# A gated cross-attention kernel on one core: own queries and keys projected for two batches at once

## The reference, cut to what matters

```
x = x + tanh(g_xattn[1]) * L1_xattn(layernorm(x), ctx)       # ctx: 16 x 361 x 256
def L1_xattn(x, xa, ...):                                    # 16 heads of width 16
    q, k, v    = split(x  @ Wqkv     + bqkv)                 # own queries, keys, values: 100 a batch
    qa, ka, va = split(xa @ Wqkv_aux + bqkv_aux)             # context keys and values: 361 a batch
    p  = softmax(q @ k.T  / sqrt(16));  pa = softmax(q @ ka.T / sqrt(16))
    out = p @ v * (1 - gate) + pa @ va * gate
    return out @ Wo + bo
```

## Time and profile before

| what | value |
|---|---|
| median of three runs | 1337.34 us (1335.42 to 1337.89) |
| the profiled execution | 1332.8 us, span 1331.1 us |
| PE, DVE, ACT, POOL busy over the span | 89%, 45%, 37%, 31% |
| second attention's step, from t = 3 to t = 13 | about 23.4 us |
| PE busy between 640 and 926 us | 281.21 of 286 us, granted clock 0.99 |

### The profile page before, as it was taken

One profiled execution on the slowest core, in us unless ns is written; L12 is line 12 of the kernel. 1 busy time (PEld: TensorE's weight loads), 2 busy tenths in 40 slices (PEclk: granted clock), 3 DMA queues, 4 the chain that ended last, 5 costly groups with the idle time before them and its releaser, 6 DMA issues.

```text
span 1331.1 us, 29074 instructions
## 1 busy us (share of the span) xinstructions
PE 1183.8 (89%) x11408; PEld 919.2 (69%) x11408; DVE 598.1 (45%) x1351; ACT 486.7 (37%) x1143; POOL 411.9 (31%) x428
## 2 busy tenths in 40 slices
PE   5999999866999999668899999999989979999960
PEld 3667777645999999535566666666656769999960
DVE  4777776752201101364566666565453402222215
ACT  2445555412333232123444444444442212233321
POOL 3666666612222221211001100110110225555532
PEclk9999999967999999957899999999989989999985
DMA  5011114017999997401100101000000129999965
GB/s 165 24 39 32 30 31 124 8 38 285 335 325 320 332 332 285 138 25 37 45 13 19 31 13 30 19 19 2 8 14 27 53 91 350 352 351 354 337 236 167
DMA packets 64352, 180.92 MB, mean 136 GB/s; under 512 B 10137, under 2 KB 36569, under 8 KB 55769
## 3 DMA queue, kind: packets, MB, share of 16 engines
q1 hardware_dynamic: 56008, 155.07, 34.2%
q0 software_dynamic: 8064, 22.03, 4.5%
q10 hardware_dynamic: 144, 1.97, 0.4%
HBM read 163.11 MB, written 15.93 MB: 135 GB/s over the span
## 4 chain that ended last, share of the span: by engine, by line
PE 67%; POOL 11%; issue 9%; DVE 7%; DMA 3%; ACT 1%; SPq 1%; POOLq 0%; DVEq 0%; ACTq 0%
PE kept_psum L1982 16%; PE kept_psum L1991 15%; POOL at_sum L316 6%; PE kept_psum L1222 5%; PE kept_psum L1278 5%; PE kept_psum L2007 4%; PE kept_psum L1242 4%; PE kept_psum L1675 4%; PE kept_psum L1264 3%; PE kept_psum L1191 3%; PE kept_psum L1206 3%; POOL at_sum L319 2%; DVE at_negmax L961 2%; PE kept_psum L1971 1%; POOL at_vn L327 1%
## 5 line engine op out<-in xcount | busy, mean ns | idle before, releaser
L1934 ACT ACTIVATE ex_hT<-kept_psum,ex_w 128x128 f32<-128x128 f32 x464 | 132.3, 368 | 309.2 <-PE kept_psum L1982 309.2
L1982 PE MATMUL kept_psum<-ex_xT,ex_w 128*128 128x128 f32 x1856 | 223.7, 277 | 0.0
L1982 PEld LDWEIGHTS kept_psum<-ex_xT,ex_w 128*128 128x128 f32 x1856 | 216.9, 194 | 0.1
L1991 PE MATMUL kept_psum<-ex_w,ex_hT 128*128 128x256 f32 x928 | 214.0, 380 | 0.0
L1991 PEld LDWEIGHTS kept_psum<-ex_w,ex_hT 128*128 128x128 f32 x928 | 170.5, 191 | 19.3
L1769 POOL DMA_INDIRECT ex_results<-ex_yt,ex_to_row x84 | 82.8, 986 | 256.1 <-DVE ex_yt L1907 256.1
L1104 ACT ACTIVATE at_probs<-kept_psum 120x800 f32<-120x800 f32 (+2 forms) x128 | 101.2, 842 | 85.2 <-PE kept_psum L1248 85.1
L961 DVE TENSOR_REDUCE at_negmax<-kept_psum 100x2 f32<-100x722 f32 x128 | 115.3, 901 | 0.0
L520 ACT ACTIVATE at_probs<-kept_psum 120x800 f32<-120x800 f32 (+1 forms) x96 | 80.2, 836 | 71.8 <-PE kept_psum L632 71.6
L1907 DVE TENSOR_TENSOR ex_yt<-kept_psum,ex_b 128x256 f32<-128x256 f32 x32 | 13.6, 424 | 200.6 <-PE kept_psum L1991 200.6
L1764 POOL DMA_INDIRECT ex_xt<-ex_normed,ex_from_row x84 | 81.5, 970 | 68.9 <-DVEq L1896 32.8
(11 more groups left out here) (239 smaller groups left out, 1782.7 us busy)
## 6 DMA issues: line engine op xcount, KB each, us to landing
ex_w<-in_pack_in SPq DMA_DIRECT2D x32, 1028.0 KB, 6.1
ex_w<-in_pack_out SPq DMA_DIRECT2D x32, 1024.0 KB, 7.6
ex_w<-in_pack_in SPq DMA_DIRECT2D x52, 514.0 KB, 5.3
ex_w<-in_pack_out SPq DMA_DIRECT2D x52, 512.0 KB, 6.1
at_ctx<-in_ctxT SPq DMA_DIRECT2D x32, 361.0 KB, 3.5
ex_normed<-ex_xhat SPq DMA_DIRECT2D x16, 200.0 KB
ex_xhat<-ex_results SPq DMA_DIRECT2D x8, 400.0 KB
ex_shT<-ex_results SPq DMA_DIRECT2D x8, 400.0 KB
```

The costliest lines, as they stand in the source:

```text
L1934: last = act.activation(hT[t % N][:, c, :], ps_h[:, (t * U + u) % N, i * P:(i + 1) * P], ACT.Gelu, bias=w1[t % N][:, B1 + c:B1 + c + 1])
L1982: last = pe.matmul(ps_h[:, (t * U + u) % N, i * P:(i + 1) * P], w1[t % N][:, c * ff + f:c * ff + f + P], xT[t % N][:, c, :], start=(c == 0 ...
L1991: last = pe.matmul(ps_y[:, t % N, 0:D], hT[t % N][:, c, :], w2[t % N][:, c * D:(c + 1) * D], start=(c == 0), stop=(c == FC - 1))
```

## The change

Own queries and keys are projected in even steps only, for batches t+2 and t+3 together. The ring's order gets `xT` twice in a row (t+2 and t+3, ahead of `sum_aux`), and `own` becomes two uses, `queries` at the old place and `own_keys` after `value01`. Each is half of the blocks, with 200 moving columns instead of 100. In odd steps none of these uses exists. On ScalarE both `take_xT` stand where the one stood, `take_queries` (four activations of 200 columns) stands at the place of `take_own`, and `take_own_keys` (two activations of 200 columns) behind the exponents of unit 2. The buffers of keys and queries go from three to four and lie in one tile each, those of xT hold two batches each, two of them. `Early` projects the context keys of four batches instead of three, so key0 and key1 start with batch 4, in step t = 2.

```diff
-EARLY_BYTES = 40960
+EARLY_BYTES = 44672
 class Early:
-    NC, NK = 4, 3
+    NC, NK = 4, 4
...
-    ORDER = (("max", 0), ("key0", 2), ("key1", 2), ("sum_main", -1), ("turn_main", -2), ("xT", 2), ("sum_aux", -1),
-             ("turn_aux", -2), ("own", 2), ("value01", 0), ("mixT", -2), ("value2", 0), ("out", -2),
+    ORDER = (("max", 0), ("key0", 2), ("key1", 2), ("sum_main", -1), ("turn_main", -2), ("xT", 2), ("xT", 3), ("sum_aux", -1),
+             ("turn_aux", -2), ("queries", 2), ("value01", 0), ("own_keys", 2), ("mixT", -2), ("value2", 0), ("out", -2),
              ("value_own", 0))
...
+    OF_TWO = ("xT", "queries", "own_keys")
+    def used(name, t, off):
+        if name in OF_TWO and t % 2:
+            return False
+        return on(t + off) and (name, t + off) not in ahead and not (name in ("key0", "key1") and t + off < NK)
...
+        def take_queries(p):
+            act.wait_ge(ready["queries"], p + 1)
+            act.wait_ge(masks_set, 4)
+            need(act, by_key_ready, (2 * p + 2 - NK) * UNITS)
             for i in range(KC):
                 for a in range(2):
-                    act.activation(qz[b % NK][:, i, a, :], bank[:, i * T:(i + 1) * T], ACT.Identity, bias=bqm[:, i, a:a + 1], scale=own[:, a:a + 1])
+                    last = act.activation(qz[:, two_of(p), i, a, :], by_two("queries", p, i), ACT.Identity, bias=bqm[:, i, a:a + 1], scale=own[:, a:a + 1])
+            last.then_inc(taken["queries"], 1)
+
+        def take_own_keys(p):
+            act.wait_ge(ready["own_keys"], p + 1)
+            need(act, by_key_ready, (2 * p + 2 - NK) * UNITS)
             for i in range(KC):
-                last = act.activation(kT[b % NK][:, i, 0:T], bank[:, (KC + i) * T:(KC + i + 1) * T], ACT.Identity, bias=bqk[:, KC + i:KC + i + 1])
-            last.then_inc(taken["own"], 1)
+                last = act.activation(kT[:, two_of(p), i, 0:T], by_two("own_keys", p, i), ACT.Identity, bias=bqk[:, KC + i:KC + i + 1])
+            last.then_inc(taken["own_keys"], 1)
...
-            if on(t + 2):
+            if on(t + 2) and t % 2 == 0:
                 take_xT(t + 2)
+                take_xT(t + 3)
             if on(t - 1):
                 take_sum(t - 1, 1)
-            if on(t + 2):
-                take_own(t + 2)
+            if on(t + 2) and t % 2 == 0:
+                take_queries((t + 2) // 2)
...
             if on(t):
                 exponents(t, 2)
+            if on(t + 2) and t % 2 == 0:
+                take_own_keys((t + 2) // 2)
...
+        def project_two(name, p):
+            bank = into(name, p)
+            first_of = KC * ("queries", "own_keys").index(name)
+            if name == "queries":
+                pe.wait_ge(taken["xT"], 2 * p + 2)
+            for i in range(KC):
+                at = (first_of + i) * P
                 for c in range(KC):
-                    last = pe.matmul(bank[:, i * T:(i + 1) * T], w[:, c, i * P:(i + 1) * P], xT[b % NX][:, c, :], start=(c == 0), stop=(c == KC - 1))
-            last.then_inc(ready["own"], 1)
+                    last = pe.matmul(bank[:, i * 2 * T:(i + 1) * 2 * T], w[:, c, at:at + P], xT[p % (NX // 2)][:, c, :, :].rearrange("p b t -> p (b t)"),
+                                     start=(c == 0), stop=(c == KC - 1))
+            last.then_inc(ready[name], 1)
...
-            if on(t + 2):
+            if on(t + 2) and t % 2 == 0:
                 turn_x(t + 2)
+                turn_x(t + 3)
...
-            if on(t + 2):
-                project_own(t + 2)
+            if on(t + 2) and t % 2 == 0:
+                project_two("queries", (t + 2) // 2)
             if on(t):
                 by_key(t, 2)
             if on(t) and t >= PRE:
                 values01(t)
+            if on(t + 2) and t % 2 == 0:
+                project_two("own_keys", (t + 2) // 2)
```

More of the change, by code:

```diff
@@ L726, in __init__ @@
         self.ctxt = [m.sb(f"ctx{i}", [P, KC, S]) for i in range(self.NC)]
-        self.kT = [m.sb(f"kT{i}", [P, KC, T + S]) for i in range(self.NK)]
+        self.kT = m.sb("kT", [P, self.NK, KC, T + S])
         self.ctx_loaded = [m.sem(f"ctx_loaded{i}") for i in range(self.NC)]
@@ L815, in attend1 @@
     HH, HS = H // HALVES, H // STRIPS
-    NC, NK, NX, PRE = early.NC, early.NK, 3, 2
+    NC, NK, NX, PRE = early.NC, early.NK, 4, 2
+    TWOS = B // 2
     KEYS = T + S
@@ L828, in attend1 @@
     xhat = [m.sb(f"xhat{i}", [T, D]) for i in range(2)]
-    xT = [m.sb(f"xT{i}", [P, KC, T]) for i in range(NX)]
-    qz = [m.sb(f"qz{i}", [P, KC, 2, T]) for i in range(NK)]
+    xT = [m.sb(f"xT{i}", [P, KC, 2, T]) for i in range(NX // 2)]
+    qz = m.sb("qz", [P, NK, KC, 2, T])
     shift = m.sb("shift", [P, HS, T], BF16)
@@ L842, in attend1 @@
     rden_ready, mixed_ready, mix_ready = m.sem("rden_ready"), m.sem("mixed_ready"), m.sem("mix_ready")
-    ORDER = (("max", 0), ("key0", 2), ("key1", 2), ("sum_main", -1), ("turn_main", -2), ("xT", 2), ("sum_aux", -1),
-             ("turn_aux", -2), ("own", 2), ("value01", 0), ("mixT", -2), ("value2", 0), ("out", -2),
+    ORDER = (("max", 0), ("key0", 2), ("key1", 2), ("sum_main", -1), ("turn_main", -2), ("xT", 2), ("xT", 3), ("sum_aux", -1),
+             ("turn_aux", -2), ("queries", 2), ("value01", 0), ("own_keys", 2), ("mixT", -2), ("value2", 0), ("out", -2),
              ("value_own", 0))
-    ready = {n: m.sem(f"{n}_ready") for n, _ in ORDER}
-    taken = {n: m.sem(f"{n}_taken") for n, _ in ORDER}
-    x_ready = taken["out"]
+    OF_TWO = ("xT", "queries", "own_keys")
     STEPS = range(-2, B + 4)
     ahead = [(n, b) for b in range(PRE) for n in ("value01", "value2")]
-    ring = ahead + [(n, t + off) for t in STEPS for n, off in ORDER if on(t + off) and (n, t + off) not in ahead
-                    and not (n in ("key0", "key1") and t + off < NK)]
+    def used(name, t, off):
+        if name in OF_TWO and t % 2:
+            return False
+        return on(t + off) and (name, t + off) not in ahead and not (name in ("key0", "key1") and t + off < NK)
+    ring = ahead + [(n, (t + off) // 2 if n in OF_TWO[1:] else t + off) for t in STEPS for n, off in ORDER if used(n, t, off)]
+    ready = {n: m.sem(f"{n}_ready") for n in dict(ORDER)}
+    taken = {n: m.sem(f"{n}_taken") for n in dict(ORDER)}
+    x_ready = taken["out"]
     ring_at = {use: i for i, use in enumerate(ring)}
@@ L1077, in take_key @@
             need(act, by_key_ready, (b - NK + 1) * UNITS)
-            act.activation(kT[b % NK][:, i, T:KEYS], ring_bank(name, b)[:, 0:S], ACT.Identity, bias=bka[:, i:i + 1]).then_inc(taken[name], 1)
+            act.activation(kT[:, b % NK, i, T:KEYS], ring_bank(name, b)[:, 0:S], ACT.Identity, bias=bka[:, i:i + 1]).then_inc(taken[name], 1)
         def take_xT(b):
@@ L1082, in take_xT, with two_of, by_two @@
             need(act, ready["value_own"], b - NX + 1)
-            act.activation(xT[b % NX][:, :, :], ring_bank("xT", b)[:, 0:KC * T].rearrange("p (c t) -> p c t", c=KC),
+            act.activation(xT[b // 2 % (NX // 2)][:, :, b % 2, :], ring_bank("xT", b)[:, 0:KC * T].rearrange("p (c t) -> p c t", c=KC),
                            ACT.Copy).then_inc(taken["xT"], 1)
-        def take_own(b):
-            act.wait_ge(ready["own"], b + 1)
+        def two_of(p):
+            return slice(2 * p % NK, 2 * p % NK + 2)
+        def by_two(name, p, i):
+            return ring_bank(name, p)[:, i * 2 * T:(i + 1) * 2 * T].rearrange("p (b t) -> p b t", t=T)
+        def take_queries(p):
+            act.wait_ge(ready["queries"], p + 1)
             act.wait_ge(masks_set, 4)
-            need(act, by_key_ready, (b - NK + 1) * UNITS)
-            bank = ring_bank("own", b)
+            need(act, by_key_ready, (2 * p + 2 - NK) * UNITS)
             for i in range(KC):
                 for a in range(2):
-                    act.activation(qz[b % NK][:, i, a, :], bank[:, i * T:(i + 1) * T], ACT.Identity, bias=bqm[:, i, a:a + 1], scale=own[:, a:a + 1])
+                    last = act.activation(qz[:, two_of(p), i, a, :], by_two("queries", p, i), ACT.Identity, bias=bqm[:, i, a:a + 1], scale=own[:, a:a + 1])
[3 more added lines that the diff above has]
+            need(act, by_key_ready, (2 * p + 2 - NK) * UNITS)
             for i in range(KC):
-                last = act.activation(kT[b % NK][:, i, 0:T], bank[:, (KC + i) * T:(KC + i + 1) * T], ACT.Identity, bias=bqk[:, KC + i:KC + i + 1])
-            last.then_inc(taken["own"], 1)
+                last = act.activation(kT[:, two_of(p), i, 0:T], by_two("own_keys", p, i), ACT.Identity, bias=bqk[:, KC + i:KC + i + 1])
+            last.then_inc(taken["own_keys"], 1)
         def exponents(b, u):
@@ L1211, in by_query @@
             if u == 0:
-                pe.wait_ge(taken["own"], b + 1)
+                pe.wait_ge(taken["queries"], b // 2 + 1)
+                pe.wait_ge(taken["own_keys"], b // 2 + 1)
                 if b < NK:
@@ L1221, in by_query @@
                 rows = slice(32 * strip, 32 * strip + 32)
```

(8 more changed lines are left out.)

2 lines of the change are left out of this document (1 added, 1 removed).

## The result

The changed kernel takes 1342.8 us in the median of eight runs, the kernel before 1335.9 in eight runs beside it: a ratio of 1.0054, 95% interval 1.0032 to 1.0076, so slower by 7 us (4 to 10). The forecast was +8.2 us, and the profile after shows the two waits where they were expected.

The account below looks back on a forecast made before the run. TensorE's list of groups was taken to bound the kernel. Steps 2 to 13 at +8.9 us, step 1 at -1.9 and steps -2 to 0 at +1.2 gave +8.2, so 1345.5 us, range 1336 to 1351.

Parts of the forecast that it names:

- The even steps' wait: In steps 2, 4 to 12 sum_aux waits for ScalarE's copy of xT, 1.40 us longer than before.
- The odd steps' wait: In steps 3, 5 to 13 k2 waits for VectorE's maxima; q2 to k2 takes 2.44 us, the step saves 1.18.
- a pair's +1.5 us: Even plus odd step: 1.4 us waiting for ScalarE, 1.0 for VectorE, 0.6 saved, half a microsecond no longer overlapped.
- The projection group: Eight TensorE instructions of 200 columns take 1.56 us, bounds 0.93 and 1.92; a pair of batches saves 0.60 us.
- The sum: Steps 2 to 13: six even steps at +2.66 us and six odd at -1.18 give +8.9 us.
- Steps -2 to 1: Start of the second attention: steps -2 to 0 cost +1.2 us, step 1 gains 1.9 us.
- another clock in steps -2 to 2: Sign of a wrong prediction: TensorE's clock in these steps differs from the one assumed, 0.50 in steps -2 to 0.
- the start runs at a better clock: Rival: denser TensorE in steps 0 and 2 raises the clock sooner, 3 to 8 us off the forecast; 15 in 100.
- key0 gives nothing: Step 1: k0 waits for VectorE anyway, so removing key0 saves no time.
- The falling clock: Rival: new gaps drop TensorE's clock in the six even steps, +18.6 us on top, 1364 us; 10 in 100.
- Step 14: Already without xT and own, used as the model for odd steps; no cost of its own in the sum.
- The total: Whole kernel: +8.2 us, 1345.5 us on the median of 1337.3; routing and experts only move with the attention.

Follow-up runs that it names:

- experiment 1: The changed kernel with the second xT of an even step moved behind sum_aux, in the ring, on TensorE and on ScalarE: ratio 1.0012 to the kernel before.
- experiment 4: The kernel before with only xT moved ahead of turn_main, in the ring and on TensorE, in every step: ratio 1.0338.
- Experiment 2: The changed kernel with the first half of value01 moved ahead of k2 in steps without a projection: ratio 0.9987 to the kernel before.
- experiment 3: The changed kernel with both the second xT behind sum_aux and value01 split around k2: ratio 0.9983 to the kernel before, 0.9971 when repeated.
- Experiments 4 to 6: experiment 4; the same with ScalarE's copy of xT between the halves of exponents(1), 1.0141; the changed kernel with three short copies ahead of take_xT, 1.0120.
- early keys alone: The kernel before with early keys of four batches and four buffers, nothing else: ratio 0.9995.

## Why the prediction was right

**The even steps' wait** was sized at 1.40 us and measured 1.35; experiment 1 shows it as a cause by taking it out, and experiment 4 by adding it to the kernel before, where a shorter one came along. **The odd steps' wait** for VectorE's maxima, read off step 14 at 2.44 us, is 2.39; an odd step gains 1.23 us where 1.18 was forecast. Experiment 2 shows that there was idle time to fill. (In the forecast's account of a pair's +1.5 us the last part should be the transposes' 0.32, not half a microsecond: 1.40 + 1.0 - 0.60 - 0.32 = 1.48. The sum doesn't use it.)

**The projection group** was the mis-sized term: eight instructions of 200 columns take 753.46 to 754.91 = 1.45 us, not 1.56. The straight line between 100 and 256 columns was too high in the middle. So the pair saved 0.8 us rather than 0.6. In the queries' place 0.1 of it is lost again: value01 starts 1.16 behind k2, not 1.05, since it has caught up with VectorE's normalization, which ends at 756.01; value01's own 1.82 us, not 1.92, give that back. From q2 to q3 it is 7.32 us against 7.53 in the forecast. An even step costs 2.40 instead of 2.66.

**The sum** over steps 2 to 13 came to +6.1 us instead of +8.9: six even steps at 0.26 less each make 1.6 of that, the odd ones 0.3, and steps 2 and 3 are a further 0.8 below the pattern.

**Steps -2 to 1** were forecast at -0.7 us together and measured -1.6, but not for the reasons given. The forecast kept the clock there as it was and named another clock in steps -2 to 2 as a sign of being wrong, and that sign came: the clock moved. In the windows of the changed kernel it is

```profile
604.00:616.00 12.00, 10.02 (x77) 0.85 0.01 2
617.00:628.00 11.00, 7.53 (x88) 0.54 0.21 56
```

and k0 of step 1, first in the changed kernel, then in the kernel before:

```profile
619.45 1.67 PE L1267 MATMUL kept_psum<-at_qz,at_kT 32*100 32x200 f32 x16 [4.03 <-DVE at_negmax L968]
621.83 0.94 PE L1242 MATMUL kept_psum<-at_qz,at_kT 32*100 32x200 f32 x16 [2.35 <-DVE at_negmax L961]
```

The clock rose at about 608 us, in step 0, whose queries and own_keys stand close together, where the kernel before had 0.50 up to 616. Step 0 was 3.8 us shorter. Then in step 1 TensorE waited 4.03 us between q0 and k0 for VectorE and went on at 0.5, and step 1 was 4.4 us longer. The rival "the start runs at a better clock" was half right; it was given back one step later. With key0 gone, nothing of TensorE's is left to fill that wait. The other traces bear this out. In all seven traces with the early keys of four batches (counting the repeat of experiment 3) TensorE waits 4.03 us there and k0 then takes 1.67 us, and step 1 is 27.3 to 30.8 us long; in the three with three batches it waits 1.5 to 2.4 us, k0 takes 0.94, and step 1 is 25.4 to 26.0. So the forecast's "key0 gives nothing" left out a loss: without key0 the wait is longer, and each time the clock is down behind it. Step 0 is 25.6 to 27.9 us in the six traces of kernels that project in pairs and 27.2 to 29.9 in the other four. That fits a gain by the pairing, but the ranges overlap.

**The falling clock** had 10 in 100. In the steady part it did not come: from 672 to 930 us the clock is 1.00, though TensorE is busy for only 245.09 of 258 us. Experiments 4 to 6 show how near it was: 0.7 us more of waiting brought it in three of six steps.

**Step 14** was taken as untouched and is 1.5 us longer, at a clock of 0.66 between 935 and 940 us. Here the clock did fall, and not in one trace alone. In all eight in which steps 2 to 13 are changed the mean clock of step 14 is 0.93 or 0.86, and the step is 1.5 or 2.6 to 2.8 us longer; in the kernel before and with early keys alone it is 1.00, and the step takes 21.82 us. TensorE's idle times ahead of k0 and q1, 1.35 and 1.02 us, are the same in the kernel before, so these waits alone don't bring the fall; what in the steps ahead does stays open. Behind step 14, too, those eight take longer, 388.3 to 392.9 us to the end against 387.5 and 386.0, and the one cause seen is the clock (0.81 against 0.89 in the result's section).

**The total** is nearer than its parts. The terms of the sum, steps -2 to 13, came to +4.5 us on the two traces, not +8.2. The medians differ by 6.9. Step 14 and what follows it, both put at nothing in the forecast, are 1.5 and 2.9 us longer on the traces and can make up the difference. So the causes in the steady part were right, and that the total came out within 1.3 us of the forecast is in part luck.

## What to carry to other kernels

In a ring of buffers the cost of an entry isn't only its own work but also whose reader the next entries then wait for. Before two uses are put side by side, list for each use which engine frees the bank two places back, and what that engine has queued ahead of the freeing instruction. And work that is taken off the bounding engine is only a gain where the group behind it wasn't waiting anyway: a step of the old kernel that lacks the same work (here the pipeline's last one) tells what is left.

## What the runs showed of the hardware

The price of a wait on TensorE was not its length alone. With one and the same group of 96 instructions behind it in steps 2 to 13, an idle time of 0.95, 1.16 or 1.39 us left it at 2.28 us; 1.69 to 1.74 us left it there in three cases of six; after 1.89 and 2.35 us it took 3.7 to 3.9 us in nine cases of twelve, at a granted clock of 0.56 in step 6. Nor did the length of one wait decide: step 14 has waits of 1.35 and 1.02 us in every trace, and the clock fell there in eight and stayed at 1.00 in two. The Trainium skill (TensorE: Matmul & The Clock Gate, A second HAM failure mode: psum-queue depth-cycling) tells of a kernel whose TensorE idles briefly between groups while it cycles through PSUM banks and keeps changing between its two clocks. Experiment 4 agrees, with nine slow sums that make 14.5 of its 42 us; the changed kernel, whose idle times are shorter, does not before step 14.

ScalarE's copies grow little with their columns: the four scaled ones took 1.41 us at 100 columns, one batch, and take 1.74 at 200, two batches.
